# Last batch's back transform by plain products, two small VectorE steps on GpSimd, fewer filler products, new instruction order

## The reference, cut to what matters

```python
xn = _layernorm(x, axis=-1)                      # x is (8, 512, 128)
# branch s
u, v = jnp.split(silu(xn @ uv_w), 2, axis=-1)
y = irfft(rfft(a, n=1024, axis=0)[None] * rfft(v, n=1024, axis=1), n=1024, axis=1)[:, :512]
s = (u * y) @ o_w                                # a: filter, from _rpe(positions), decayed
# branch g
rw = softmax(xn.mean(axis=1) @ Wr + br)          # one row for a batch
tk_w, tk_i = top_k(repeat(rw, 512), 2); tk_w = softmax(tk_w)
h = gelu(einsum('nd,edf->enf', xn, W1) + b1)     # only the two picked experts count
out = sum over picked experts of tk_w * (h @ W2 + b2)
g = silu(layernorm(out + xn) * gamma + beta)
x = x + s * g
```

## Time and profile before

| what | us |
|---|---|
| median of 3 runs | 187.89 (187.7 to 188.25) |
| the profiled execution, own time | 187.92 |
| its span, first to last instruction | 186.1 |
| TensorE busy | 181.3 (97%) |
| VectorE / ScalarE / GpSimd busy | 131.1 / 122.4 / 132.4 |

### The profile page before, as it was taken

One profiled execution on the slowest core, in us unless ns is written; L12 is line 12 of the kernel. 1 busy time (PEld: TensorE's weight loads), 2 busy tenths in 40 slices (PEclk: granted clock), 3 DMA queues, 4 the chain that ended last, 5 costly groups with the idle time before them and its releaser, 6 DMA issues.

```text
span 186.1 us, 3992 instructions
## 1 busy us (share of the span) xinstructions
PE 181.3 (97%) x1270; PEld 166.3 (89%) x1270; DVE 131.1 (70%) x439; ACT 122.4 (66%) x246; POOL 132.4 (71%) x136
## 2 busy tenths in 40 slices
PE   7999999999999999999999999999999999999992
PEld 7988889999987878998998999999999999999991
DVE  2898998889562589439696398099169980885594
ACT  0379899999987999585638554956355555664500
POOL 1404755656798254897999979998998789788350
PEclk9999999999999999999999999999999999999999
DMA  5158047324083052011032041307000510002103
GB/s 163 35 147 253 3 124 222 97 60 113 12 280 108 0 149 79 0 58 60 0 103 67 0 116 56 113 16 201 14 0 6 168 56 0 5 0 60 56 0 113
DMA packets 20988, 14.48 MB, mean 78 GB/s; under 512 B 1416, under 2 KB 18496, under 8 KB 20968
## 3 DMA queue, kind: packets, MB, share of 16 engines
q1 hardware_dynamic: 20320, 13.87, 25.7%
q10 hardware_dynamic: 648, 0.37, 0.6%
HBM read 12.14 MB, written 2.10 MB: 76 GB/s over the span
## 4 chain that ended last, share of the span: by engine, by line
PE 86%; DMA 5%; DVE 4%; SPq 2%; issue 1%
PE bank L1304 30%; PE bank L1137 9%; PE bank L1139 8%; PE bank L1138 8%; PE bank L1318 7%; PE bank L1365 7%; DMA x_all<-in_L_attn_x 5%; PE bank L1385 4%; PE bank L1204 3%; PE bank L1360 2%; DVE stats L813 1%; PE bank L1185 1%; PE bank L1310 1%; PE bank L1247 1%; PE bank L1220 1%
## 5 line engine op out<-in xcount | busy, mean ns | idle before, releaser
L1304 PEld LDWEIGHTS bank<-w_s,h_ring 128*128 128x128 f32 x512 | 64.4, 191 | 3.0 <-issue 0.2
L1304 PE MATMUL bank<-w_s,h_ring 128*128 128x128 f32 x512 | 66.3, 275 | 0.0
L617 ACT ACTIVATE h_ring<-bank,b_sel 128x512 f32<-128x512 f32 (+1 forms) x72 | 45.5, 641 | 30.9 <-PE bank L1139 23.6
L1137 PE MATMUL bank<-xT_hi,w_hi 128*128 128x512 f32 (+1 forms) x72 | 31.3, 435 | 0.0
L1139 PE MATMUL bank<-xT_hi,w_lo 128*128 128x512 f32 (+1 forms) x72 | 26.6, 370 | 0.0
L1138 PE MATMUL bank<-xT_lo,w_hi 128*128 128x512 f32 (+1 forms) x72 | 26.4, 367 | 0.0
L1003 DVE TENSOR_TENSOR prod<-bank,Qre 128x512 f32<-128x512 f32 x24 | 16.5, 687 | 13.3 <-PE bank L1318 7.7
L731 POOL TENSOR_TENSOR w_lo<-w_raw,w_hi 128x512 fp32r<-128x512 f32 x15 | 19.1, 1280 | 3.9 <-ACT w_hi L586 3.9
L759 POOL TENSOR_TENSOR Y<-prod 128x512 f32<-128x512 f32 x16 | 20.1, 1278 | 0.6
L1318 PE MATMUL bank<-fold,fwd_sb 128*128 128x256 f32 x64 | 16.4, 379 | 0.0
L1006 DVE TENSOR_TENSOR prod<-bank,Qim 128x512 f32<-128x512 f32 x24 | 16.3, 680 | 0.0
(11 more groups left out here) (176 smaller groups left out, 375.5 us busy)
## 6 DMA issues: line engine op xcount, KB each, us to landing
w_raw<-in_L_ffn_W SPq DMA_DIRECT2D x16, 256.0 KB, 2.7
w_s<-in_L_ffn_W SPq DMA_DIRECT2D x16, 256.0 KB, 3.2
x_all<-in_L_attn_x SPq DMA_DIRECT2D x7, 256.0 KB, 3.9
out_dram<-x_all SPq DMA_DIRECT2D x7, 256.0 KB, 2.3
Y<-table_lag SPq DMA_DIRECT2D x1, 512.0 KB, 5.2
fwd_sb<-table_fwd SPq DMA_DIRECT2D x1, 256.0 KB, 4.8
inv_sb<-table_inv SPq DMA_DIRECT2D x1, 256.0 KB, 4.9
out_dram<-x_all SPq DMA_DIRECT2D x2, 128.0 KB, 1.8
```

The source lines that it names most:

```text
L617: nc.scalar.activation(h_ring[:, n % NH, tok], H_PS[n % 2][:, tok], ACT.Gelu, bias=b1_sel[:, i, c:c + 1]).then_inc(h_done, 1)
L1137: nc.tensor.matmul(out_ps_ap, w_hi, m_hi, start=True, stop=False)
L1304: last = nc.tensor.matmul(OUT_PS[u][:, tok], h_ring[:, n % NH, tok], w2_s[:, i % NW2, c], start=(n % HT == 0 and t == t0), stop=(n % HT == ...
```

## The change

- `rw` (position weights) and the larger part of `pick` (the pick of b1's column for each expert) go from VectorE to GpSimd. There the two sums that VectorE made in one reduction are made by halving: five additions in `rw`, three in `pick`. The indices' conversion and the one-hot rows stay on VectorE as a job `hot`, with a semaphore `hot_done`; `coef` now waits for that and not for the pick.
- `DIRECT` goes: units 7 and 8 take the plain form, four products each (eight for the batch), with `odd` on ScalarE and `eo` on VectorE. `negate_sine` goes.
- By the tables, `warm` keeps seven jobs: 17 filler products in place of 31.
- All five tables have new places.

```diff
-DIRECT = 7
 SP_AT = {
-    "x": [0, 1, 7, 9, 10, 12, 17, 21],
+    "x": [0, 1, 3, 8, 10, 15, 16, 21],
...
 PE_AT = {
-    "warm": [0, 1, 2, 3, 9, 10, 11, 12, 13, 14, 15, 16, 19, 20, 22, 23, 25, 26, 29, 30, 32],
+    "warm": [0, 1, 2, 3, 6, 8, 9],
...
-    "back": [136, 145, 167, 179, 195, 223, 241, 244, 246],
+    "back": [122, 130, 148, 170, 181, 203, 220, 225, 231],
...
-            def negate_sine(n):
-                act_e.wait_ge(lo_pool, lo_count(NTILE - 3))
-                act_e.wait_ge(inv_in, 16)
-                nc.scalar.activation(minus_sin, inv_sb[:, :, 1], ACT.Copy, scale=-1.0).then_inc(minus_done, 1)
...
+            def position_weights(n):
+                pool.wait_ge(rpe_in, 16 * 8)
+                pool.wait_ge(consts_in, 16)
+                nc.gpsimd.tensor_copy(rows32.rearrange("r (g j) -> r g j", g=RG),
+                                      bcast(rows8.unsqueeze(1), [8, RG, R]))
+                step(nc.gpsimd.tensor_tensor(l0c[:, 0:16], l0[:, 0:16], l0[:, 16:32], ALU.add))
+                for n in (8, 4, 2):
+                    step(nc.gpsimd.tensor_tensor(l0c[:, 0:n], l0c[:, 0:n], l0c[:, n:2 * n], ALU.add))
+                step(nc.gpsimd.tensor_tensor(lmean[:, 0:1], l0c[:, 0:1], l0c[:, 1:2], ALU.add))
+                step(nc.gpsimd.tensor_scalar(lmean[:, 1:2], lmean[:, 0:1], -1.0 / R, None, ALU.mult))
+                step(nc.gpsimd.tensor_scalar(l0c, l0, lmean[:, 1:2], None, ALU.add))
...
+            def bias_pick(g):
+                first, end = GROUPS[g]
...
+                pool.wait_ge(hot_done, g + 1)
...
+                step(nc.gpsimd.tensor_tensor(
+                    pick[:, 0:m], bcast(hot[:, i0:i1].unsqueeze(2), [P, m, FC, E]),
+                    bcast(b1T[:].unsqueeze(1), [P, m, FC, E]), ALU.mult))
+                for n in (4, 2):
+                    step(nc.gpsimd.tensor_tensor(pick[:, 0:m, :, 0:n], pick[:, 0:m, :, 0:n], pick[:, 0:m, :, n:2 * n],
+                                                 ALU.add))
+                nc.gpsimd.tensor_tensor(b1_sel[:, i0:i1], pick[:, 0:m, :, 0], pick[:, 0:m, :, 1],
+                                        ALU.add).then_inc(b1_done, 1)
...
             def convolved(u):
                 b, t0, t1 = UNITS[u]
-                if u < DIRECT:
-                    dve.wait_ge(eo_done, u + 1)
-                else:
-                    dve.wait_ge(eo_ps, u + 1)
+                dve.wait_ge(eo_done, u + 1)
...
-                        if u >= DIRECT:
-                            for part in range(2):
-                                for kc in range(2):
-                                    wave = minus_sin[:, kc] if part * ri else inv_sb[:, kc, part]
-                                    last = nc.tensor.matmul(EO_PS[u][:, o:o + P], Y[:, q % 2, kc, n, part, s],
-                                                            wave[:, ::-1] if ri else wave,
-                                                            start=(part + kc == 0), stop=(part + kc == 2))
-                            continue
```

More of the change, by code:

```diff
@@ L92 @@
     "set": [0],
[L93 removed]
+    "xroot": [1, 2, 7, 10, 14, 15, 24, 26],
     "uvw": [3],
[L95 to L101 removed]
[3 rows of a table removed]
[L105 removed]
+    "rw": [4],
+    "pick": [5, 17, 21, 34],
@@ L167 @@
-    "back": [136, 145, 167, 179, 195, 223, 241, 244, 246],
-    "s": [146, 155, 175, 194, 221, 235, 245, 247, 248],
+    "wr": [7],
+    "b1t": [10],
+    "logits": [11, 21, 42, 86],
+    "pv": [12, 16, 29, 45, 59, 75, 84, 87],
+    "pu": [14, 17, 31, 43, 60, 79, 82, 88],
+    "rows": [15],
[7 rows of a table added]
+    "out": [27, 35, 36, 37, 40, 41, 52, 53, 55, 58, 62, 64, 69, 70, 74, 76, 93, 96, 98, 101, 104, 106, 107,
[3 rows of a table added]
+    "phi": [77],
+    "cs": [80],
+    "re": [83, 89],
+    "im": [85, 91],
+    "f0": [90, 103, 117, 131, 146, 165, 182, 194],
```

194 lines of the change are left out of this document (85 added, 109 removed), and 50 rows, old and new, of tables (DVE_AT, PE_AT, POOL_AT).

## The result

| what | before | after |
|---|---|---|
| median, us | 187.98 (187.67 to 188.28, 6 runs) | 190.53 (189.04 to 191.35, 6 runs) |
| ratio | | 1.0121, 95% interval 1.0086 to 1.0156 |
| the profiled execution, own time | 187.92 | 191.35 |
| its span | 186.1 | 189.6 |

The change makes the kernel slower, by 2.5 us in the median and 3.4 us in the profiled executions. The forecast of 187.8 was wrong, and the time lies outside its range (186.3 to 189.7). The changed kernel also spreads more: its six runs, with the mean granted clock of each, are 189.04 (0.994), 189.73 (0.993), 190.09 (0.995), 190.97 (0.985), 191.27 (0.987) and 191.35 (0.974). Medians in this document are of all runs, ratios leave out the runs that lie over 1.5% above the fastest of their kernel.

A forecast was written before the change was run, and what follows sets the result against it. TensorE's summed products were taken to bound the kernel from 22 us to the last expert product. From 187.92 us, front -0.1, middle 0, moved transform +0.89 and tail -0.9 gave -0.1: 187.8 us, range 186.3 to 189.7.

The forecast's parts named there:

- What bounds the kernel: Whole kernel: from 22 us to the last expert product, TensorE's summed products set the time; only front and tail can move.
- The direct back transforms: Units 7 and 8 at the end: unit 7's moved transform makes the last `out` issue 0.89 us later.
- The tail: From the last `out` issued (T) to the end: 7.0 us before, 6.1 after, so -0.9 us.
- The front: Start of the kernel up to `h` of tile 4: -0.1 us, bounds -1.3 and +1.5.
- Its walk: Step-by-step times for the start of the new kernel: `h` of tile 0 at 17.3 us, tile 4 at 23.2.
- rival 3: Front: TensorE's clock falls in the gaps, lower level from 15 to 20 us; +2.5, 190.3 us; chance 0.03.
- The 14 filler products give nothing by themselves: Front: dropping these TensorE products gains nothing by itself, as real work or a wait stands in their place.
- The middle: The 150 us with new rows on every engine, where TensorE waited nowhere before: 0 taken, up to +1.5 us.
- Rival 2: GpSimd becomes late in the middle, 93% busy from 100 to 140 us; one miss 1.3 us, 189.1; chance 0.18.
- `rw` and `pick` at 0: Front: moving these two jobs to GpSimd costs 0 us; the upper end costs 0.1 to 0.5.
- the tail's two terms: End of the kernel: +0.89 us for unit 7's transform ahead of the last `out`, -0.9 from there to the end.

The follow-up runs named there:

- B: The kernel before with one edit: with 14 filler products left out 188.22 us, ratio 0.9992; with both `rw` and `pick` on GpSimd 189.90 us, ratio 1.0091.
- A: The changed kernel, unchanged or with one further edit; timed again unchanged, 191.36 us, ratio 1.0128 to the kernel before.
- the pieces: The changed kernel with GpSimd's one long filter-weights product (`wc`) cut into seven instructions; 189.55 us, ratio 1.0039 to the kernel before.

## Why the prediction was wrong

- **What bounds the kernel** was right: the front and the end move, the sum of TensorE's products stands between them. But "busy at the full clock in every slice" was read as a property of the kernel. It was one of this execution and of its order: one in six timed runs of the kernel before has a fall, and eight in ten without the fourteen fillers.
- **The direct back transforms**, +0.89: right.
- **The tail**, -0.9: right, measured -1.0, step by step: `o` at T + 0.20 (forecast 0.25), variance at 1.48 (1.5), affine steps at 2.60 (2.7), end at 5.98 (6.1).
- **The front**, -0.1: a step that failed; it measured +1.8. Its walk held within half a microsecond up to `h` of tile 0 as long as the clock was full (17.3 against 16.88). What failed is the rule behind it, that durations at full clock may be used in a front with waits of 1.5 and 1.2 us. That was named, as rival 3 (the text above calls it the last), priced at 190.3 with the fall at 15 to 20 us, and given 0.03, though no row of the kernel before shows TensorE at full clock behind such waits. The fall came at 8 to 16 us, and `h` of tile 4 came 1.9 us later than forecast in the profiled execution.
- **"The 14 filler products give nothing by themselves"**: true for B's median (188.22 against 188.20), but with a reason that the prediction did not have: a gain of some 0.4 us at full clock (by two runs only) and a loss by the clock.
- **The middle**, 0 with a bound of +1.5: the other failed step. "Before, TensorE waits nowhere there" was taken for room. Before, the normalisation stood in the same way; only what was queued behind it differed. Measured +1.5, the bound itself. That the bound holds is luck: the prediction derived it from nothing, and named no stall of VectorE.
- **Rival 2** had the right engine and the wrong mechanism. GpSimd was not late; it held VectorE. And 100 to 140 us, where it is 93% busy, has no wait (40.00 of 40 us after too); the wait is where GpSimd has one long instruction.
- **`rw` and `pick` at 0**: right in A's order by its trace, wrong as a statement on the edit: 1.7 us in B's, in part by the same stall.
- **The combination.** Front and middle were summed with one likeliest value each, and no rival had both losses in it. 187.8 + 1.5 + 1 to 2 us for the clock gives 190.3 to 191.3, and 190.53 and 191.36 were measured. With the pieces, A took 187.91 in the one run of ten at a clock of 0.998: close to the forecast, in a kernel that needed both mended.

What stays open: why the clock sometimes outlasts a wait of 1.70 us and sometimes falls behind 1.03 or less; the last 0.3 us of the account; why the kernel with filler in all waits is fastest in runs with a lower clock; and whether the tail's two terms can be had without a new wait in the kernel before.

## What to carry to other kernels

Filler that costs nothing may be what keeps the clock up; if an edit makes a wait in a front that had none, price every product of the next ten microseconds at both levels, and run it often enough to see the spread. Before a step is queued on VectorE beside GpSimd, look at how long GpSimd's longest instruction there is, even if the step is tiny: cut that instruction to pieces (of 0.6 us here), or keep nothing behind VectorE's step that TensorE needs soon. When a step with a wait is moved to another engine, what counts is not its length but what stands behind it in that row: one pick at a wrong place cost 10 us.
